# Adding the first level of a sum over keys on VectorE, in the second layer's recurrences alone

## The chip, the cores and the metric

One core of a Trainium2 chip runs the whole kernel. The metric is the device time in microseconds (us) of one launch; the table below gives the median of three runs. PE is TensorE's matmul side, PEld its weight loads, DVE VectorE, ACT ScalarE, POOL GpSimd.

## What is computed

Four layers run over x of shape 16 x 128 x 256 (16 sequences of 128 steps, 256 channels). The first and third are RWKV blocks, the second and fourth attend to a context of 128 positions. The part that the change touches is the recurrence of the RWKV block, with 32 heads of 8 keys s by 8 values t:

```
def step(s, inp):
    k_l, v_l, w_l, r_l = inp
    a = k_l[..., :, None] * v_l[..., None, :]
    out = jnp.einsum('bhs,bhst->bht', r_l, faaaa * a + s)
    s_new = a + w_l[..., None] * s
    return (s_new, out)
_, outs = jax.lax.scan(step, s0, seq)
```

The output of a step is a sum over the 8 keys of r times the state. After it come a group norm, a gate, the projection `Wo` and the block's channel mix.

## The kernel before

The 16 sequences are worked in four groups of four. `STEPS` lists eight steps: the first kernel layer (one RWKV block and one attention) for groups 0 to 3, then the second kernel layer for groups 0 to 3. In the second, the recurrence's unit is of kind `mixer_ffn` and the attention's unit is of kind `attn_mlp`; "the second layer" below is always this second half, some 504 to 1008 us of the profiled span, with a tail of attention and MLP behind it.

Each step is cut into three programs that run side by side, like a software pipeline: `head` (norm, token shift, projections of the next unit), `recurrence` (of this unit) and `attn` (of the unit before). They share the engines. Every engine runs its instructions strictly in the order in which they were issued, and that order is a table: `ORDER` holds for each engine a string of the letters H, R and A, and `in_order` takes the next piece (up to a `yield`) of the head, recurrence or attention program for each letter. So a piece that waits holds back all pieces behind it on its engine.

A recurrence unit has 128 partitions for 4 sequences x 32 heads. It works through the 8 values in `NCH` = 4 chunks of `DC` = 2 values. For each chunk c:

- VectorE forms the outer product k*v in `A_[c % 2]` (`outer`, L473, 128 x 2032),
- runs two scans over key and time, `S_` = w*S + A (L563, 128 x 1024 each),
- multiplies by r: `A_[c % 2]` = `R_` * `S_` (L571, 128 x 2048), and raises `r_rs`;
- TensorE waits for `r_rs` and adds the 8 keys up in PSUM: `RS` = 8 matmuls with the identity (L1301, 128 x 256 each), then raises `r_y`. Each such fp32 matmul stands in the trace as two instructions.

The outer product of chunk c+2 waits for `r_y`, since it writes the same buffer. After the last chunk ScalarE squares the result (L913), VectorE forms the group norm's sums and scales (L585, L588, L590, L592), TensorE transposes (L1079) and projects with `Wo` (L1129).

Beside the recurrence lies attention: TensorE makes the scores of 16 jobs per unit in two alternating banks (L1380), VectorE takes their negative maximum (`nmax`, L659), ScalarE the exponentials (L1003), TensorE transposes them (L1393) and forms the values (L1404). It begins with the queries, which VectorE scales (L654) and a DMA spreads into `QX`. GpSimd makes the reciprocal standard deviations of the layer norms (L767, L768) for VectorE's L421 and the copy L513 before it, and one product of the recurrence (L786).

Of the kernel before, what the change touches and what calls it, by code (L numbers as in the profile page):

```python
# [8 lines left out]
ALU = mybir.AluOpType  # L9
# [11 lines left out]
RH, RS = 32, 8  # L21
# [8 lines left out]
DC = 2  # L30
# [69 lines left out]
for _group in range(G):  # L100
# [2 lines left out]

ORDER = {
    "VectorE":
        "HHHHHHHHHHHHAHHRRHHRRRRRRRRRRRHRHHRRRHHRHHHRRRRHHRRAAHHAARRHAAHAAARARRHHARRAARRAARARRARAAHRAHAARAHRR"
        "HAAAHARRRARRHAHHAARARAAHHAAHHAAAHHRARAARRRRAARRAARARAHARAHRAAARRAARRRHAHAAHRHHRRHAARHHRAARHAHRAAAAAH"
        "HAAAHHRARHHRAARHHRHRAHHARAHRHAHARARARRRARAHHAARRRAAAAHHAARRRRARAHHRRARAAAARAAHHRRRRAAARAHHRHAARHHRRA"
        "RRRAARARRAAHRAHRRRRAHHARARRARAHHARRAAAAAHHRAARRAAARARRRAARRARAAHHARARRARRAHARHAARRHRAAHAHRRRRARAAHHR"
        "RRARAHHARRAAHHAARHHRRRRRRAAARRAARAARAARARAHHAARRHAHARAAAHRRRHHAAAARHHARRRAARAHHARRARHHRRRHRRRAAHRAAA"  # L110
        "RRARARAARARARARARARRARAAARRRAAAHHRARRRAHRHARHRARRARRAHHAHRRAAAAAAAHAAHAHAAAAAAAAAAAAAAAHHHAAAAH",
    "GpSimd":
        "HRRHAARRHAARRHAARHRARAHRRRARHRARAHRARARRHRAHAHHA",
    "ScalarE":
        "HHHHHHHHHHHRRRHHRRHRHRHHHHAHHAAAAHHRAAAAAAAAAAARAAAAHAAAAAARAAAAARAHARAAARAAHAARAAAAAHHHAHHAAAHHHAHR"
        "AAAAAAAARAAAAAAAAAAAAAAAAARHAAARRHARAHAARHAAHAAAAAAAHHHAAAHHHRAHAHAAAHAHAAAAARAAAAAHAAHAAARAAAAAHHHA"
        "AAARRARAHHARAAAAAAAAARHHAAAHAAAHRAAAHRAAAAARAAARARAAHHARHAAAAAHHAAAARAHHAAAARAARRAAAAAAHRHAAAAAAAAAA"
        "ARAAAAAHAAARAAAAAHRAARARAHRAAAAHHAAARAHAAHHAAARHRHRAAARHHAAAAAAAAAAARAAAAAAAHAAAAAAAARAAAHRRAHAAARAH"
        "AAAAARAAHHAHHARRAHHAAARRRAAHAHAAAAAAAAAAAAARAAAAAAARAAARAAARARAHAARAAAHAHHAAARRRARAAHAAHAAAAHAAAAAAA"
        "AAAAAAAAAAHAAAAAAHHAAAAAAAAAAAAHAHAAAAHA",  # L120
    "TensorE":
        "HHHHHHHHHHHHHHHHHHHHHHHRHRRRRRRHRRRRHRRRRRRHHHHHRHRHHRHHHHAHHAHAHAAAHHAAHHAHAHAAAAHRRARAAAARRAAHAAAA"
        "RRAAARARAAAAARRRRAAAAHAARRRRAAHHAAAAAHRHARRAHAAAHHHAHHAAHAHAAHHHHAHHAAAAAAAHRHRAARAAHRHAAAAARAAAARAA"
        "HRARAAAAAHRAAARRAARRRRRRHAAHHAHHARHAHAHAHARAAARAHAHAAHAHAAHHAHHHHAHHHHAHHAAAAHRARHHAHAHARAAARHAAAAAA"
        "RARHRARARHHARAAAARRAHHRAHAAHAARRRRAAHHAAHARHAARARAAAAHAHHHHHAAAAARRARHHAAAHRRAARARAHRHAARHRRRARAAHAA"
        "RRARRAAAHAAAHRHAHRRHAAAHAAHHRAAHHAAAARAAHARHAARRAARAHAHAAAAAHAAAHHAARHRAARRAAAAAHAAAARHARARRRRRAAAAR"
        "ARAAHARRRRAHAAAHARHHRRAAHAHAHAHARAHAHAHAAHRRRAHHRRHAHAAHHAAAAAAAAAHRHRARRAHAAAARHAARAAAAAAAHHARRARAA"
        "AAARRAARAAHAARRRRRHHAHAHAAHAAAHARARAHAHRAHHAHAHAHRAHRRARHAHRRAAAHAHAAAAAAAARRAAARRAAHAAAARAARARAHRHA"
        "ARAHRARRRAAAAARRRRAHAAHAARAARRHAHAHHRHHAAHARRRARAAAHAAARAHHAAHAHAHAAHAAAAAAAAAAAAAAAHAAAAAHAHAAAAAHH"
        "HAAAAAAAHAAAHAHAHHAHAAAAAAHH",  # L130
}


# [17 lines left out]
def build(nc, x, ctx, ctx_t, s0, state, mask_row, mask_col, rwkv_w, attn_w, mlp_w, bias_w, common, out):  # L151
# [5 lines left out]
    with ExitStack() as stack:  # L157
        def sb(name, shape, dt=F32):
            return stack.enter_context(nc.sbuf_tensor(name, [P] + shape, dt))
# [149 lines left out]
        sem = {n: stack.enter_context(nc.semaphore(n)) for n in names}  # L309
# [10 lines left out]
        with nc.Block() as block:  # L320
# [78 lines left out]
            def _(dve):  # L399
                v = nc.vector  # L400
# [146 lines left out]
                def recurrence(u):  # L547
                    xf = X2[u.lane][:].rearrange("p b c -> p (b c)")
                    yield
                    dve.wait_ge(sem["r_turned"], u.at("r_turned", 6))  # L550
                    link(outer(u, 0))
                    yield
                    link(outer(u, 1))
                    yield
                    dve.wait_ge(sem["r_rk"], u.at("r_rk", 1))
                    v.tensor_reduce(RU[:], YT[:].rearrange("p k t -> p t k"), AX.X, ALU.add).then_inc(sem["r_ru"], 1)
                    for c in range(NCH):
                        yield
# [12 lines left out]
                        v.tensor_tensor(A_[c % 2][:], R_[:].unsqueeze(1).broadcast_to([P, DC, RS, T]), S_[:], ALU.mult)\  # L571
                            .then_inc(sem["r_rs"], 1)
                        dve.wait_ge(sem["r_rs"], u.at("r_rs", c + 1))
                        if 1 <= c < NCH - 1:
                            yield
                            last = outer(u, c + 1)
                            if c == NCH - 2:
                                last.then_inc(sem["r_out"], 1)
                                dve.wait_ge(sem["r_out"], u.at("r_out", 1))
                            else:  # L580
                                link(last)

# [24 lines left out]
                    if u.kind == "mixer_ffn":
                        yield from channel_mix(u, "g", in_mixer, 1)
# [463 lines left out]
            def _(pe):  # L1072
# [211 lines left out]
                def recurrence(u):  # L1284
                    pb = lambda h: PB[:, h * 512:(h + 1) * 512]
                    for c in range(NCH):
                        if c == NCH - 1:
                            yield
                            pe.wait_ge(sem["r_vr"], u.at("r_vr", 1))
                            for h in range(HALF):  # L1290
                                last = t.matmul(pb(h), ident, V_[:, h * RS // 2:(h + 1) * RS // 2], start=False, stop=False,
                                                skip_group_check=True)
# [2 lines left out]
                        yield  # L1295
                        pe.wait_ge(sem["r_rs"], u.at("r_rs", c + 1))
                        y = PB[:, DC * c * T:DC * (c + 1) * T]
                        for k in range(RS):
                            if k and k % 2 == 0:
                                yield  # L1300
                            last = t.matmul(y, ident, A_[c % 2][:, :, k], start=(c % 2 == 0 and k == 0), stop=False,  # L1301
                                            skip_group_check=True)
# [273 lines left out]
```

## Time and profile before

| | before |
|---|---|
| median of three runs | 1144.96 us (1141.52 to 1145.21) |
| the profiled execution's own time | 1146.65 us |
| its span | 1144.7 us |
| TensorE matmul busy | 1032.4 us (90% of the span) |
| TensorE weight loads busy | 774.9 us (68%) |
| VectorE busy | 780.4 us (68%) |
| ScalarE busy | 536.1 us (47%) |
| GpSimd busy | 109.5 us (10%) |
| mean granted TensorE clock | 0.966 |

Busy is the time in which at least one instruction of the engine ran. The span is the time from the first to the last instruction of the profiled execution; 1.95 us of that execution's time lie around it.

### The profile page before, as it was taken

How to read it: one execution, taken by the hardware profiler on the slowest of the kernel's cores; microseconds unless marked ns; L12 is line 12 of the kernel's file. 1: busy time of each engine (PE TensorE's matmuls, PEld its weight loads, DVE VectorE, ACT ScalarE, POOL GpSimd, SP SyncE). 2: the span in 40 equal slices, each digit the busy share in tenths (PEclk: the TensorE clock that was granted, in tenths of full speed). 3: DMA queues.
4: the chain of work that ended last, by engine and by line, in shares of the span. 5: the costliest groups of instructions: out<-in, count | busy, mean ns of one | idle time of the engine just before them, and what ended most of it. 6: DMA issues, size and time to landing. Idle time of an engine off the chain costs nothing. (4 is left out here: it accounts for less than half of the span.)

```text
span 1144.7 us, 21376 instructions
## 1 busy us (share of the span) xinstructions
PE 1032.4 (90%) x8866; PEld 774.9 (68%) x8866; DVE 780.4 (68%) x1078; ACT 536.1 (47%) x1643; POOL 109.5 (10%) x101
## 2 busy tenths in 40 slices
PE   7846889989998889978999989998999979999998
PEld 5634567766676657765667667785777757787777
DVE  3597759866996589779975688746986479532330
ACT  1102326743655235552476446642672445734762
POOL 1001010101010020002100202010100010000000
PEclk9967999989999899999999989999999989999999
DMA  9200000000000010000000000001000010000000
GB/s 371 87 0 1 2 25 16 1 2 20 21 2 2 1 32 10 1 2 19 17 6 2 20 20 2 2 2 41 9 1 2 11 38 3 1 1 21 27 10 19
DMA packets 17058, 24.80 MB, mean 22 GB/s; under 512 B 4417, under 2 KB 13761, under 8 KB 16322
## 3 DMA queue, kind: packets, MB, share of 16 engines
q1 hardware_dynamic: 16962, 23.44, 6.2%
q8 instruction: 70, 1.15, 0.4%
q14 instruction: 26, 0.21, 0.1%
HBM read 17.13 MB, written 2.10 MB: 17 GB/s over the span
## 5 line engine op out<-in xcount | busy, mean ns | idle before, releaser
L1003 ACT ACTIVATE big<-QB,nmax 128x128 f32<-128x128 f32 x512 | 181.6, 376 | 110.4 <-DVE nmax L659 109.2
L1301 PE MATMUL PB<-A,common_w 128*128 128x256 f32 x512 | 132.0, 399 | 21.7 <-DVE A L571 21.7
L563 DVE TENSOR_TENSOR_SCAN S_<-W_,A 128x1024 f32<-128x1024 f32 x64 | 146.5, 2311 | 0.3
L1380 PE MATMUL QB<-big,QX 128*128 128x256 f32 x512 | 135.7, 388 | 10.7 <-DMA QX<-big 10.7
L1301 PEld LDWEIGHTS PB<-A,common_w 128*128 128x128 f32 x512 | 97.8, 199 | 43.2 <-DVE A L571 26.7
L659 DVE TENSOR_REDUCE nmax<-QB 128x4 f32<-128x512 f32 x128 | 86.2, 683 | 54.0 <-PE QB L1380 52.7
L1380 PEld LDWEIGHTS QB<-big,QX 128*128 128x128 f32 x512 | 99.9, 196 | 30.3 <-DMA QX<-big 12.2
L1003 ACT ACTIVATION_READ_ACCUMULATOR big<-QB,nmax 128x1 f32 x512 | 110.2, 215 | 0.0
L1267 PE MATMUL PA<-X,rwkv_w 128*32 128x128 f32 x3072 | 100.9, 289 | 10.1 <-DVE X L458 9.8
L449 DVE SCALAR_TENSOR_TENSOR PA<-PA,rwkv_w,SX 128x512 f32<-128x512 f32 x80 | 56.5, 752 | 70.3 <-PE PA L1184 65.5
L1267 PEld LDWEIGHTS PA<-X,rwkv_w 128*32 128x32 f32 x3072 | 88.4, 117 | 22.3 <-DVE X L458 15.6
L1393 PE MATMUL QA<-common_w,big 128*128 128x128 f32 x512 | 78.6, 276 | 3.6 <-ACT CN L1012 2.2
L1393 PEld LDWEIGHTS QA<-common_w,big 128*128 128x128 f32 x512 | 60.8, 141 | 24.7 <-issue 16.3
L473 DVE TENSOR_TENSOR A<-K_,V_ 128x2032 f32<-128x2032 f32 x32 | 72.4, 2263 | 2.1 <-PE PB L1301 1.7
L571 DVE TENSOR_TENSOR A<-R_,S_ 128x2048 f32<-128x2048 f32 x32 | 73.2, 2287 | 0.6
L1375 PE MATMUL QB<-mrow,first_row 128*128 128x512 bf16 x128 | 49.8, 389 | 9.1 <-ACT big L1003 7.4
L1012 ACT ACTIVATE XT<-QA 128x512 f32<-128x512 f32 x64 | 38.7, 605 | 29.0 <-PE QA L1393 28.8
L458 DVE TENSOR_TENSOR X<-PA,XN 128x512 f32<-128x512 f32 x80 | 51.5, 685 | 1.2
L1184 PE MATMUL PA<-low,rwkv_w 32*128 32x256 f32 x256 | 44.8, 425 | 7.3 <-ACT K_ L892 1.9
L1129 PE MATMUL QA<-attn_w,CT 128*128 128x256 f32 x192 | 45.3, 382 | 4.5 <-DVE CT L678 4.5
L1012 ACT ACTIVATE CN<-QA 128x512 f32<-128x512 f32 x64 | 38.8, 606 | 20.1 <-PE QA L1393 19.8
L1129 PE MATMUL PB<-rwkv_w,S_ 128*128 128x256 f32 x192 | 45.4, 385 | 1.1 <-DVE S_ L598 1.0
(192 smaller groups left out, 1720.4 us busy)
## 6 DMA issues: line engine op xcount, KB each, us to landing
rwkv_w<-in_rwkv_w SPq DMA_DIRECT2D x2, 2866.0 KB, 14.9
QX<-big SPq DMA_DIRECT2D x128, 32.0 KB, 1.9
attn_w<-in_attn_w SPq DMA_DIRECT2D x2, 1031.5 KB, 17.2
mlp_w<-in_mlp_w SPq DMA_DIRECT2D x1, 2052.0 KB, 23.4
X<-in_x SPq DMA_DIRECT2D x4, 512.0 KB, 16.8
ctx<-in_ctx SPq DMA_DIRECT2D x4, 512.0 KB, 3.4
ctx<-in_ctx_t SPq DMA_DIRECT2D x4, 512.0 KB, 3.4
out<-XT SPq DMA_DIRECT2D x4, 256.0 KB, 2.0
```

What stands on the lines that cost most here:

```text
L449: last = v.scalar_tensor_tensor(pa4(h), pa4(h), r_pack[u.layer][:, col:col + 1], SX[:, h], ALU.add, ALU.mult)
L473: return v.tensor_tensor(A_[c % 2][:, :, :, 1:T], K_[:, :, 0:T - 1].unsqueeze(1).broadcast_to([P, DC, RS, T - 1]), V_[:, DC * c:DC * c + D ...
L563: last = v.tensor_tensor_scan(S_[:, d].rearrange("p k t -> p (k t)"), W_[:].rearrange("p k t -> p (k t)"), A_[c % 2][:, d].rearrange("p k ...
L571: v.tensor_tensor(A_[c % 2][:], R_[:].unsqueeze(1).broadcast_to([P, DC, RS, T]), S_[:], ALU.mult)\
L659: v.tensor_reduce(nmax[:, n % 2], bank(2 + n % 2).rearrange("p (j s) -> p j s", j=JH), AX.X, ALU.max, negate=True).then_inc(sem["a_max"], 1)
L1003: last = s.activation(PR[:, n % 2, j], bank(2 + n % 2)[:, j * T:(j + 1) * T], ACT.Exp, bias=nmax[:, n % 2, j:j + 1], accum_out=den[:, b, h ...
L1012: s.activation(PT[n % QUAD], bank(0).rearrange("p (j t) -> p j t", j=JH), ACT.Copy)\
L1129: last = t.matmul(dst[:, (b - base) * C:(b - base + 1) * C], lhs(h, b), w[:, h], start=(h == 0 and b == 2 * k), stop=(h == HALF - 1 and bi ...
L1267: last = t.matmul(PA[RH * b:RH * b + RH, k * T:(k + 1) * T], wt[:, h, RH * k:RH * k + RH], src[:, h, b * T:(b + 1) * T], start=(h == 0), s ...
L1301: last = t.matmul(y, ident, A_[c % 2][:, :, k], start=(c % 2 == 0 and k == 0), stop=False, skip_group_check=True)
L1380: last = t.matmul(o, QX[b % 2][:, i, h], K2[:, :, h, b * T:(b + 1) * T], start=False, stop=True, skip_group_check=True)
L1393: last = t.transpose(bank(0)[:, j * T:(j + 1) * T], PR[:, n % 2, j], ident)
```

## The change

In units of kind `mixer_ffn`, VectorE adds keys 4 to 7 to keys 0 to 3 in place, behind the product with r, and only then raises `r_rs`. TensorE then adds 4 keys instead of 8. All other units stay as they were. The new addition stands behind a `yield` of its own, so that the table can put other pieces between the product and it.

```diff
-                        v.tensor_tensor(A_[c % 2][:], R_[:].unsqueeze(1).broadcast_to([P, DC, RS, T]), S_[:], ALU.mult)\
-                            .then_inc(sem["r_rs"], 1)
+                        last = v.tensor_tensor(A_[c % 2][:], R_[:].unsqueeze(1).broadcast_to([P, DC, RS, T]), S_[:], ALU.mult)
+                        if u.kind == "mixer_ffn":
+                            link(last)
+                            yield
+                            part = A_[c % 2]
+                            last = v.tensor_tensor(part[:, :, 0:RS // 2], part[:, :, 0:RS // 2], part[:, :, RS // 2:RS], ALU.add)
+                        last.then_inc(sem["r_rs"], 1)
                         dve.wait_ge(sem["r_rs"], u.at("r_rs", c + 1))
...
-                        for k in range(RS):
+                        for k in range(RS // 2 if u.kind == "mixer_ffn" else RS):
                             if k and k % 2 == 0:
                                 yield
                             last = t.matmul(y, ident, A_[c % 2][:, :, k], start=(c % 2 == 0 and k == 0), stop=False,
```

`link` raises VectorE's own semaphore and waits for it, so the addition starts when the product has been written.

The strings of `ORDER` are new on every engine that has one, in the first layer too. Their first line for VectorE:

```diff
     "VectorE":
-        "HHHHHHHHHHHHAHHRRHHRRRRRRRRRRRHRHHRRRHHRHHHRRRRHHRRAAHHAARRHAAHAAARARRHHARRAARRAARARRARAAHRAHAARAHRR"
...
+        "HHHHHHHHHHAHHHHRRHHRRRRRRRRRRRHRHHRRRHHRHHHRRRRHHRRAAHHAARRHAAHAAARRRRHARAHARARAARRARARAHAARHAAHRRR"
...
```

The string of VectorE is 16 letters longer (595 to 611) and that of TensorE 32 shorter (828 to 796): 16 additions more, and two pieces of two matmuls less in each of the 16 chunks. Three places show what the new order does. Names of lines behind L575 are 5 higher in the changed kernel (`nmax` is L664 there, the matmuls over keys L1306); its addition is L576.

VectorE, the end of group 3's recurrence in the second layer. Before:

```order
L563 SCALAR_TENSOR_TENSOR S_<-W_,A 128x1024
L571 TENSOR_TENSOR A<-R_,S_ 128x2048
L671 RECIPROCAL rden<-den 128x32
L473 TENSOR_TENSOR A<-K_,V_ 128x16x127
L659 TENSOR_REDUCE nmax<-QB 128x4
L678 TENSOR_TENSOR CT<-QA,az 128x2x2x128
L659 TENSOR_REDUCE nmax<-QB 128x4
L563 SCALAR_TENSOR_TENSOR S_<-W_,A 128x1024 x2
L571 TENSOR_TENSOR A<-R_,S_ 128x2048
L687 TENSOR_TENSOR X<-QA,X 128x512
```

Now:

```order
L571 TENSOR_TENSOR A<-R_,S_ 128x2048
L576 TENSOR_TENSOR A<-A 128x2x512
L676 RECIPROCAL rden<-den 128x32
L473 TENSOR_TENSOR A<-K_,V_ 128x16x127
L664 TENSOR_REDUCE nmax<-QB 128x4
L683 TENSOR_TENSOR CT<-QA,az 128x2x2x128
L664 TENSOR_REDUCE nmax<-QB 128x4
L563 SCALAR_TENSOR_TENSOR S_<-W_,A 128x1024 x2
L571 TENSOR_TENSOR A<-R_,S_ 128x2048
L692 TENSOR_TENSOR X<-QA,X 128x512
L664 TENSOR_REDUCE nmax<-QB 128x4
L576 TENSOR_TENSOR A<-A 128x2x512
```

Here the update of X (L687, now L692) and one more `nmax` stand ahead of the last addition, and otherwise only the additions are new.

VectorE, the start of group 2's recurrence in the second layer (its first scans, and the start of attention beside it). Before:

```order
L571 TENSOR_TENSOR A<-R_,S_ 128x2048
L563 SCALAR_TENSOR_TENSOR S_<-W_,A 128x1024
L654 TENSOR_SCALAR big<-QA,attn_w 128x512 x2
L563 SCALAR_TENSOR_TENSOR S_<-W_,A 128x1024
L659 TENSOR_REDUCE nmax<-QB 128x4 x2
L571 TENSOR_TENSOR A<-R_,S_ 128x2048
L659 TENSOR_REDUCE nmax<-QB 128x4 x2
L473 TENSOR_TENSOR A<-K_,V_ 128x16x127
```

Now:

```order
L576 TENSOR_TENSOR A<-A 128x2x512
L421 TENSOR_SCALAR az<-X,amv,arstd 128x256 x4
L563 SCALAR_TENSOR_TENSOR S_<-W_,A 128x1024 x2
L659 TENSOR_SCALAR big<-QA,attn_w 128x512 x2
L571 TENSOR_TENSOR A<-R_,S_ 128x2048
L576 TENSOR_TENSOR A<-A 128x2x512
L664 TENSOR_REDUCE nmax<-QB 128x4 x2
L473 TENSOR_TENSOR A<-K_,V_ 128x16x127
```

The second chunk's scans now stand ahead of the scaling of the queries (`big`), and its product and addition ahead of the first two `nmax`.

VectorE, the second chunk of group 0's recurrence in the second layer. Before:

```order
L416 BN_AGGR amv<-abn 128x2 x4
L563 SCALAR_TENSOR_TENSOR S_<-W_,A 128x1024
L421 TENSOR_SCALAR az<-ctx,amv,arstd 128x256 x4
L545 SCALAR_TENSOR_TENSOR Gt<-Gt,PA 128x1024
L413 BN_STATS bn<-X 128x6 x4
L416 BN_AGGR mv<-bn 128x2 x4
L563 SCALAR_TENSOR_TENSOR S_<-W_,A 128x1024
L513 COPY XN<-st 128x8
L421 TENSOR_SCALAR X_0<-X,mv,rstd 128x256 x4
L654 TENSOR_SCALAR big<-QA,attn_w 128x512 x2
L571 TENSOR_TENSOR A<-R_,S_ 128x2048
```

Now:

```order
L416 BN_AGGR amv<-abn 128x2 x4
L545 SCALAR_TENSOR_TENSOR Gt<-Gt,PA 128x1024
L413 BN_STATS bn<-X 128x6 x4
L416 BN_AGGR mv<-bn 128x2 x4
L421 TENSOR_SCALAR az<-ctx,amv,arstd 128x256 x4
L563 SCALAR_TENSOR_TENSOR S_<-W_,A 128x1024 x2
L513 COPY XN<-st 128x8
L421 TENSOR_SCALAR X_0<-X,mv,rstd 128x256 x4
L571 TENSOR_TENSOR A<-R_,S_ 128x2048
L576 TENSOR_TENSOR A<-A 128x2x512
L659 TENSOR_SCALAR big<-QA,attn_w 128x512
```

Both scans now stand behind the second of two batch-norm blocks and behind L421, and the scaling of the queries behind the product and the addition.

## Rows read from the trace of the kernel before

**Rows 1.** The page, part 1: busy time, share of the span, instructions of each engine.
```profile
PE 1032.4 (90%) x8866; PEld 774.9 (68%) x8866; DVE 780.4 (68%) x1078; ACT 536.1 (47%) x1643; POOL 109.5 (10%) x101
```

**Rows 2.** Groups of instructions: count | busy us, mean ns | idle us before, releaser.
```profile
L1301 PE MATMUL PB<-A,common_w 128*128 128x256 f32 x512 | 132.0, 399 | 21.7 <-DVE A L571 21.7
...
L571 DVE TENSOR_TENSOR A<-R_,S_ 128x2048 f32<-128x2048 f32 x32 | 73.2, 2287 | 0.6
...
L590 DVE TENSOR_TENSOR A<-PB,RU 128x1024 f32<-128x1024 f32 x8 | 9.8, 1225 | 0.3
...
L659 DVE TENSOR_REDUCE nmax<-QB 128x4 f32<-128x512 f32 x128 | 86.2, 683 | 54.0 <-PE QB L1380 52.7
```

**Rows 3.** Windows: the four stretches of the second layer, and 708.40 to 775.00 between two.
```profile
core 0: us, PE busy (x) PEld busy (x) DVE busy (x) ACT busy (x) POOL busy (x), PEclk, DMA share, GB/s
523.28:575.88 52.60, 48.07 (x223) 34.09 (x221) 49.86 (x58) 21.69 (x61) 8.52 (x5) 1.00 0.07 20
653.64:704.64 51.00, 44.11 (x251) 31.45 (x249) 45.48 (x45) 22.87 (x91) 7.50 (x3) 0.93 0.08 21
708.40:775.00 66.60, 65.85 (x777) 51.46 (x776) 41.74 (x67) 36.37 (x96) 6.76 (x6) 1.00 0.01 2
775.05:838.75 63.70, 59.86 (x331) 43.07 (x330) 52.06 (x62) 33.15 (x118) 6.85 (x5) 0.97 0.08 23
924.64:967.44 42.80, 38.94 (x248) 30.36 (x249) 39.51 (x28) 23.93 (x103) 2.36 (x1) 0.92 0.06 13
```

**Rows 4.** The page, part 4: the chain that ended last, by engine and line.
```profile
PE 36%; DVE 5%; ACT 3%; issue 1%; SPq 1%; POOL 1%; DMA 1%; POOLq 0%; DVEq 0%; ACTq 0%
PE QB L1380 4%; PE PB L1129 4%; PE PB L1301 3%; PE QA L1129 3%; PE PA L1267 3%; PE QA L1119 2%; PE PA L1109 2%; PE QA L1393 2%; ACT big L1003 2%; PE PA L1119 2%; PE QA L1404 1%; PE PB L1088 1%; PE QB L1109 1%; PE QB L1088 1%; PE PA L1184 1%
```

**Rows 5.** The chain in order of time (start us, us, what), second layer.
```profile
675.90 2.21 DVE A L571
...
702.45 2.21 DVE A L571
...
704.70 3.73 PE PB L1301 x16
...
838.82 3.72 PE PB L1301 x16
...
960.46 1.73 PE PB L1301 x8
...
968.88 3.47 PE PB L1301 x16
```

**Rows 6.** Timeline of VectorE, group 3: start, us, what [idle before <-releaser].
```profile
929.27 0.69 DVE L659 TENSOR_REDUCE nmax<-QB 128x4 f32<-128x512 f32 x1 [2.35 <-PE QB L1380]
...
965.15 2.29 DVE L571 TENSOR_TENSOR A<-R_,S_ 128x2048 f32<-128x2048 f32 x1
...
969.02 0.69 DVE L687 TENSOR_TENSOR X<-QA,X 128x512 f32<-128x512 f32 x1 [1.57 <-PE QA L1094]
```

**Rows 7.** Timeline of VectorE, group 1.
```profile
665.86 0.69 DVE L659 TENSOR_REDUCE nmax<-QB 128x4 f32<-128x512 f32 x1 [1.79 <-PE QB L1380]
...
671.96 0.69 DVE L659 TENSOR_REDUCE nmax<-QB 128x4 f32<-128x512 f32 x1 [2.48 <-PE QB L1380]
...
700.99 0.17 DVE L513 COPY XN<-st 128x8 f32<-128x8 f32 x1 [0.90 <-POOL rstd L768]
```

**Rows 8.** Timeline of VectorE, group 0.
```profile
538.86 1.38 DVE L421 TENSOR_SCALAR az<-ctx,amv,arstd 128x256 f32<-128x256 f32 x4 [1.12 <-POOL arstd L768]
...
546.46 0.17 DVE L513 COPY XN<-st 128x8 f32<-128x8 f32 x1 [1.18 <-POOL rstd L768]
```

**Rows 9.** Timeline of VectorE, group 2.
```profile
783.71 1.38 DVE L421 TENSOR_SCALAR az<-X,amv,arstd 128x256 f32<-128x256 f32 x4 [1.41 <-POOL arstd L768]
...
798.48 0.69 DVE L659 TENSOR_REDUCE nmax<-QB 128x4 f32<-128x512 f32 x1 [3.74 <-PE QB L1380]
...
802.91 0.69 DVE L659 TENSOR_REDUCE nmax<-QB 128x4 f32<-128x512 f32 x1 [3.73 <-PE QB L1380]
```

More of the change, by code:

```diff
@@ L105 @@
     "VectorE":
-        "HHHHHHHHHHHHAHHRRHHRRRRRRRRRRRHRHHRRRHHRHHHRRRRHHRRAAHHAARRHAAHAAARARRHHARRAARRAARARRARAAHRAHAARAHRR"
[L107 to L110, printed above, removed]
@@ L111 @@
-        "RRARARAARARARARARARRARAAARRRAAAHHRARRRAHRHARHRARRARRAHHAHRRAAAAAAAHAAHAHAAAAAAAAAAAAAAAHHHAAAAH",
+        "HHHHHHHHHHAHHHHRRHHRRRRRRRRRRRHRHHRRRHHRHHHRRRRHHRRAAHHAARRHAAHAAAARRRRHARAHARARAARRARARAHAARHAAHRRR"
+        "AAHHARARHRARARHHARRAAAAHHAAHHAAAHHARRAARRRRAARARARARAAHHARRARAARAARRRHHAAHARHHHRARRHHRAAAHHARRAAAAAH"
+        "HAAAHHRARHHRAARHHRHRAHHARHAARAHHARRRARARAARHHRAAARRAAHHAARRRRARAHHRRARAAAARAAHHRRRRRAAAHHARRHRRAHARH"
+        "RRRRARAARRARRAARAHHRRRARHHARRRARAAAHHAARRAAAHHARRRAAAARARRRAAHRAHRRAARRRAARRRAARRHRAAHRHAARRRAHAHRRR"
@@ L112 @@
+        "RAARHHARRRARHHAARAHHRAAAHHRRRRRRRRAARARRAARRAARARAHAHRRAARHARAAHRAAARHRAARHHARAHRHAARRARAHHARRARRHHR"
+        "RRARAHAHRRAARRARARRARARARRARARARARRARAAARRRAARAHHRARRRAHRHAHRRRRAARRHHHAARRAAAAAAAAHAHAAAHAAAAAAAAAA"
+        "AAHHAHAAAAH",
     "GpSimd":
-        "HRRHAARRHAARRHAARHRARAHRRRARHRARAHRARARRHRAHAHHA",
+        "HRRHAARRHAARRHAARHRARAHRRRARHRARARHARARRHRHAAHHA",
     "ScalarE":
-        "HHHHHHHHHHHRRRHHRRHRHRHHHHAHHAAAAHHRAAAAAAAAAAARAAAAHAAAAAARAAAAARAHARAAARAAHAARAAAAAHHHAHHAAAHHHAHR"
@@ L116 @@
[L116 to L120, printed above, removed]
@@ L121 @@
-    "TensorE":
[L122 to L130, printed above, removed]
+        "HHHHHHHHRHHHRRHHRHRRHRHHHHAHHAAAAHHRAAAAAAAAAAAAARAAAAHAAAAAAARAAHAARRAARAHAARAAAAAAHAHAHHHAAAHHHRAH"
@@ new lines @@
+        "AAAAAAAAAAAAAAAARAAAAAAARAAAARHRAHARAHAARHHAAAAAAAAHAHRHAAAHHHHAAHAAAHAAAAHAAAAARAHAAHAAAAAAARAAAAHR"
+        "HHAARARHHAAARAAAAAAARHAHAAAHAAHRAHAARAAAAAAARARAARAAAHHRHAAAAAHHAAAAARHHAAARAARARAAAHAHAAARAAAAAAAAA"
+        "AARAAHAAAAAARAHRAAAARAARAHRAAHAHAAARHAAHHAAAAHRARHRHAHAARAAAAAAAARAAAAAAAHAARAAAAAAAAAAAAHAARRAHRAAA"
+        "AAAHRAAHAHAHHARAARAARRHHAAAHRHAAAAAAAAAAAARAAAAAAARAAAAARAAARRAHARAAAAHAHHAAARRHAARRAAAAHAAAHAAAAAAA"
+        "AAAAAAAAAAHAAAAAAHHAAAAAAAAAAAAHAHAAAHAA",
@@ new lines @@
+    "TensorE":
+        "HHHHHHHHHHHHHHHHHHHHHHHRRRRHRRRRHRRHRRRRRRRHHHHHRHRHHRHHHHAHHAAHAHAAHHAAAAHHAHAHARRRAAARHAAAAARRAAAA"
+        "AHAARAARAARAARRAARHAAAARRRRRHHAAAAAHARAHRARAHAAAHHHAHHAAHAHAAHHHHAHHAAAHAAAARRAHRAAHAARAHAAAAAAARHAA"
+        "RARRAARRAARRRAAAHAAARRRRHAHHAAHHARHAHAARAHAHAARAHAHAHAAHAAHHAHHHHAHHHHAHHAAAAHAHHAAARRAAHAHAAARRHAAR"
+        "ARRHAAHARAHAARAARHHRAAARARAAHRHRRRAHHAAAAHRAAHRARAAAAHAHHHHHAAAAAHRRHAAAHAARHHHAHARAAAARARRAAAARRAAA"
+        "AAHAHRHAHRRHHAAAAAHARAAHAAAHHRAARARHAHAAARRAHHAHAAAAHAAHAAHAAARRAAAAHRRAAHAAAAAAAAARRHARAAARRAAAHAAH"
+        "ARHHRAHRHAAHAAHRAAHHHAHRAHHAARAHRHRRAHHAAAAAAAAAAARAARHHAAHHAAARAAAHHAARAAAAAAAAAAARRAAAAAHRRRHHAAHH"
+        "AAAAAHARHARHAAHRAHHAHAHAARAHRRRAAHRHRAHAAHHAAAAAAAARAAARAAAAHAAARRAAAAAARHAHRAHAAAARRRAAAHHARAARARHA"
+        "HHAHHHARAHARRHRHAHAAAARRAAAAAHAHAHAAHAAAAAAAAAAAAAAAAAHAAAHAHAAAAAHHHAAAAAAAHAAAAHHAHHHAAAAAAHAH",
```

## Prediction

> **What bounds the kernel now.** I began with the busy times [rows 1]: TensorE 90% of the span, VectorE 68%. Taken alone they say that TensorE is the bound and VectorE has room. The chain of waits says the same [rows 4]: TensorE holds 36% of the span there, VectorE 5%; all engines together make 48%, since this chain could be followed back through the later half only. The matmuls over keys (L1301) are 3% of the span on it, some 34 us, and that half is the second layer with its tail. But an average is taken over stages with different limits, so I looked at the stretches in which the change works. I call the time from a recurrence's first scan to its last product with r its **stretch**, and cut the trace there [rows 3]: the first, second, fourth and fifth rows are groups 0, 1, 2 and 3. The reader is to see that VectorE is busy 49.9 of 52.6 us, 45.5 of 51.0, 52.1 of 63.7 and 39.5 of 42.8, hence 95%, 89%, 82% and 92%, and TensorE 91%, 86%, 94% and 91%. In these stretches both engines are nearly full. Between two of them only TensorE is: 65.9 of 66.6 us in the third row [rows 3], VectorE 41.7. So outside the stretches TensorE sets the pace, and a stretch that ends later pushes all that is behind it; inside, whichever is fuller after the change does.
>
> **What TensorE loses.** 4 units x 4 chunks x 4 matmuls = 64 matmuls, which are 128 of the 512 instructions of the group L1301 [rows 2]. At full clock 16 instructions take 3.47 us and 8 take 1.73 [rows 5], so a chunk saves 1.73 us, a unit 6.9 and the four units 27.7 us. That is the most the change can give.
>
> **What VectorE gains.** 16 additions of 128x1024. None is in the trace. From below: half of the product's 2.29 us, 1.14. From above: the whole 2.29, if writing in place slowed it [rows 2]. Nearest is L590, a tensor_tensor of the same 128x1024: 1.225 us [rows 2]; I take 1.2, so 4.8 us a unit and 19.2 in all. The wait of `link` ahead of it I cost at nothing: between scans and product the same kind of wait stands, and that group has 0.6 us of idle before it over 32 products [rows 2]. No DMA moves.
>
> **What of it lies on the path.** In a stretch VectorE had 2.7, 5.5, 11.6 and 3.3 us of idle (span less busy) [rows 3]. The additions can only hide in that. I walked the new order of each stretch with the old durations.
>
> Group 3. Of its idle, 2.35 us stand before the first `nmax`, which waits for scores that wait for the queries' DMA [rows 6]; the order there is as before, so this stays. The other 0.9 us can go. The order shows two more pieces ahead of the last addition, the update of X and one `nmax`, 0.69 and 0.67 us long [rows 6, 2] but following each other at some 0.6 us, beside the 4.8 us of additions. The last addition then ends at 4.8 + 1.3 - 0.9 = 5.2 us past 967.44, where the last product ended. TensorE started its last chunk at 968.88, 1.4 us behind the product, being busy itself, and ended at 972.35 [rows 5]. Now it starts at 972.6 and needs 1.73: it ends at 974.4, **+2.0 us**, although it did 6.9 us less.
>
> Group 1. Its idle is 1.79 and 2.48 us before two `nmax` and 0.90 before the copy that waits for GpSimd's deviations [rows 7]. The new order fills the second; the first grows by what is put in front of it, and the third by as much as the block of batch norm moves back. I take 0.4 us less idle in all. With one more `nmax` (0.67 us a piece) [rows 2] the last addition ends 4.8 + 0.6 - 0.4 = 5.0 us late, and the last chunk, which started right at the product's end and took 3.73 us [rows 5], gives 1.73 back: **+3.3 us**. The chain runs through VectorE's products here, three of the four (the first and the last stand in [rows 5]), which says that VectorE already set this stretch.
>
> Group 0. Both waits for GpSimd, 1.12 and 1.18 us [rows 8], are filled: the new order has the second batch-norm block ahead of the first `az`, and a pair of scans ahead of the copy. One `nmax` fewer lies in the stretch. So 4.8 - 2.3 - 0.6 = 1.9 us, less 1.73 for the last chunk, 0.2; but the scaling of the queries now stands behind a product and an addition, and attention starts later by about 3 us, of which I charge 0.8: **+1.0 us**.
>
> Group 2. It has holes: 1.41 us for GpSimd, then 3.74 and 3.73 us before the first two `nmax` [rows 9]. The new order puts the first addition into the first hole and the second chunk's product and addition (3.5 us) into the next. The last addition then ends where the last product did, and the last chunk (3.72 us) [rows 5] gives 1.73 back: **-1.7 us**.
>
> The sum is 2.0 + 3.3 + 1.0 - 1.7 = +4.6 us. Against the profiled execution's own 1146.65 us (span 1144.7, 1.95 around it) that is 1151.3; that execution is 1.7 us above the median of the runs shown, so I give 1144.96 + 4.6 = **1149.6 us**. The order in the first layer is new as well; its additions and matmuls are the same in number, I see no wait that it clearly removes, and cost it at 0, with 3 us to either side.
>
> [...]
>
> **The rivals.**
>
> *TensorE sets the end in the stretches too (faster).* For it: the chain holds matmuls over keys at the end of groups 1, 2 and 3 [rows 5], and TensorE is busy 94% and 91% there; the new order puts additions into holes. Then half of the 34 us on the chain goes, 17 us, and only group 1's three products carry an addition on the chain, 3.6 us: 13.4 us faster, 1131.6. With half of that, where VectorE gives way in some stretches, 1138. Against it: VectorE is as full, and has no way to do 6 us more in 3.3 us of idle. [...]
>
> *It balances (no change).* The holes cover more than I think, above all group 1's GpSimd wait, or the new order of the first layer gives 3 us: 1142 to 1148.
>
> *The additions delay attention (slower by more).* Each `nmax` behind an addition comes 1.2 us later; ScalarE and TensorE's scores wait for it in two alternating banks. Its place is the start of attention beside each recurrence; it decides if the holes before `nmax` stay as long as before. Then all 19.2 us of additions lie on the path and only the last chunks' 4 x 1.73 = 6.9 come back: +12.3, 1157. TensorE, idler, may also drop its clock more often: it was 0.93 and 0.92 in groups 1 and 3 [rows 3]. With an addition priced at the upper bound of 2.29 us my own sum would be +17 higher, 1167, which I hold for hardly possible.
>
> **How the numbers follow.** A measurement can tell this kernel's change from none at about 0.3%, 3.4 us. Chances: my forecast 0.33, of which its spread of some 4 us leaves a part below 3.4 us; attention delayed 0.12; balance 0.20; TensorE the bound in full or in part 0.35. That gives 0.42 for slower, 0.23 for no change and 0.35 for faster. The cases have both signs: the forecast's own range is 1145 to 1155; the range that holds 8 in 10 has to reach the faster case's 1131.6 and most of the slower one's, 1131 to 1157.
>
> **What would show each step.** Right: an addition of 1.2 us; stretches of about 54, 56, 64 and 48 us, with VectorE above 90% in groups 0, 1 and 3; TensorE busy about 1005 us, and its idle before the matmuls over keys (L1306), released by VectorE, well above the 21.7 us of before [rows 2], by some 20 us; waits for GpSimd in group 0 gone. Wrong: stretches of groups 2 and 3 no longer than before, or TensorE's idle as before and the span some 15 us shorter, which would say that VectorE's rows could be packed closer than I walked them. If the additions took over 1.5 us, the price is wrong, not the place.

## The result, and the profile after

| | before | changed |
|---|---|---|
| median of six runs | 1145.09 us (1141.12 to 1145.67) | 1152.21 us (1150.32 to 1156.02) |
| ratio | | 1.0073, 95% interval 1.0059 to 1.0087 |
| profiled execution, span | 1144.7 us | 1150.0 us |
| mean granted TensorE clock | 0.966 | 0.961 |

The change makes the kernel slower by 0.7%; the forecast was 1149.6 us, slower by 0.4%. The page of the changed kernel, to be held against [rows 1]:

```profile
span 1150.0 us, 21144 instructions
...
PE 1012.0 (88%) x8738; PEld 753.7 (66%) x8738; DVE 797.1 (69%) x1094; ACT 536.4 (47%) x1643; POOL 104.8 (9%) x101
```

TensorE is busy 20.4 us less and VectorE 16.7 more. (27.7 us of matmuls at full clock were taken out; where the clock is low, an instruction's time grows, and overlapping times are counted once.) Only now read the windows. The stretches, from a recurrence's first scan to its last addition, stand here as in [rows 3], groups 0 to 3:

```profile
core 0: us, PE busy (x) PEld busy (x) DVE busy (x) ACT busy (x) POOL busy (x), PEclk, DMA share, GB/s
523.50:578.90 55.40, 47.22 (x204) 32.06 (x203) 54.76 (x62) 22.00 (x61) 4.86 (x5) 0.94 0.07 19
655.42:710.64 55.22, 39.87 (x203) 27.23 (x205) 50.89 (x50) 23.15 (x90) 5.42 (x3) 0.88 0.07 19
778.84:843.55 64.71, 57.33 (x318) 40.77 (x316) 57.52 (x68) 32.90 (x122) 7.52 (x5) 0.97 0.08 22
926.77:975.27 48.50, 36.06 (x230) 26.45 (x230) 45.70 (x34) 25.19 (x110) 2.35 (x1) 0.96 0.05 12
```

They take 55.4, 55.2, 64.7 and 48.5 us where they took 52.6, 51.0, 63.7 and 42.8: +2.8, +4.2, +1.0 and +5.7, together 13.7 us. VectorE is busy 99%, 92%, 89% and 94% of them, TensorE 85%, 72%, 89% and 74%. The engine that bounds the stretches is VectorE in groups 0, 1 and 3; in group 2 the two are level, and only the experiments tell.

What lies between them, and the tail behind the last, before:

```profile
575.88:653.64 77.76, 73.77 (x856) 56.30 (x857) 48.31 (x84) 47.10 (x147) 8.58 (x6) 1.00 0.02 4
704.64:775.05 70.41, 69.60 (x792) 54.71 (x793) 45.48 (x73) 39.13 (x107) 6.76 (x6) 1.00 0.01 2
838.75:924.64 85.89, 81.74 (x825) 59.67 (x824) 48.88 (x85) 40.44 (x99) 7.53 (x8) 1.00 0.03 11
967.44:1144.70 177.26, 169.21 (x981) 136.43 (x979) 58.89 (x125) 92.71 (x287) 7.86 (x16) 1.00 0.04 13
sum 411.32, PE 394.32 PEld 307.11 DVE 201.57 ACT 219.38 POOL 30.74; mean PE 98.58 PEld 76.78 DVE 50.39 ACT 54.85 POOL 7.68
```

and after:

```profile
578.90:655.42 76.52, 72.54 (x852) 54.80 (x853) 48.49 (x83) 46.16 (x147) 8.59 (x6) 1.00 0.02 5
710.64:778.84 68.20, 66.94 (x797) 52.16 (x790) 44.83 (x71) 38.76 (x106) 7.97 (x6) 1.00 0.01 2
843.55:926.77 83.22, 79.61 (x817) 58.21 (x816) 47.74 (x83) 40.84 (x96) 7.53 (x8) 1.00 0.04 12
975.27:1150.00 174.73, 166.13 (x965) 133.94 (x965) 57.70 (x123) 91.55 (x282) 7.72 (x16) 1.00 0.04 13
sum 402.67, PE 385.23 PEld 299.11 DVE 198.76 ACT 217.31 POOL 31.82; mean PE 96.31 PEld 74.78 DVE 49.69 ACT 54.33 POOL 7.95
```

This sum is 8.6 us shorter, and TensorE's busy time in it 9.1 us shorter. So outside the stretches the relief of TensorE comes back as time, nearly one for one. With the first scan 0.22 us later (523.50 against 523.28), 13.7 - 8.6 + 0.2 = 5.3 us, the whole difference of the spans. Those 0.2 us are no measure of the first layer's new order: in the seven kernels below whose first layer is that of before the first scan stands at 521.4 to 522.9 us, and in the four others that have the new order at 518.6 to 524.3.

The groups of the addition and of the matmuls over keys, as in [rows 2]:

```profile
L1306 PE MATMUL PB<-A,common_w 128*128 128x256 f32 x384 | 96.7, 392 | 18.4 <-DVE A L571 16.2
...
L576 DVE TENSOR_TENSOR A<-A 128x1024 f32<-128x1024 f32 x16 | 19.5, 1220 | 0.4
```

The addition takes 1.220 us, and the wait of `link` leaves 0.4 us of idle over all 16. The 128 instructions are gone (512 to 384), but the idle before the rest did not grow as the prediction said it would: 18.4 us where it was 21.7, and nearly all of both lies in the first layer (2.3 and 2.5 us in the second, in the lines below). TensorE's idle went elsewhere. Its longest waits in the second layer (504 to 1008 us; total us, times, longest), changed kernel:

```profile
PE QB L1380 <- ACT big L1008: 19.2, 21, 3.4
PE QB L1385 <- DMA QX<-big: 11.3, 3, 3.8
...
PE PB L1306 <- DVE A L576: 2.3, 3, 1.8
```

and before:

```profile
PE QB L1380 <- DMA QX<-big: 9.8, 3, 3.8
...
PE PB L1301 <- DVE A L571: 2.5, 3, 1.5
PE QB L1375 <- ACT big L1003: 2.5, 5, 1.2
```

The mask row that opens a job's scores (L1380 now, L1375 before) waits 19.2 us in all, 21 times, for the exponentials of two jobs earlier, and waited 2.5. TensorE often reached a score before attention was ready for it.

Group 1's holes of [rows 7] in the changed kernel:

```profile
667.73 0.69 DVE L664 TENSOR_REDUCE nmax<-QB 128x4 f32<-128x512 f32 x1 [2.73 <-PE QB L1385]
...
702.60 0.17 DVE L513 COPY XN<-st 128x8 f32<-128x8 f32 x1 [1.11 <-POOL rstd L773]
```

The hole before the first `nmax` grew from 1.79 to 2.73 us, the second is gone, and the wait for GpSimd went from 0.90 to 1.11. Group 0's two waits for GpSimd [rows 8] are gone. In group 3 the hole of [rows 6] stayed at its 2.35 us:

```profile
931.40 0.69 DVE L664 TENSOR_REDUCE nmax<-QB 128x4 f32<-128x512 f32 x1 [2.35 <-PE QB L1385]
```

and TensorE, which had started its last chunk there 1.4 us behind the product, now waits for the last addition:

```profile
975.33 1.99 PE L1306 MATMUL PB<-A,common_w 128*128 128x256 f32 x8 [1.80 <-DVE A L576]
```

### The profile page after: what moved, and what is told of

Its sections match the earlier page's. It is cut to its first block, busy times and chain, and to the rows that moved or that the text cites. A ratio compares the mean times of both kernels' runs of the same rounds, so it can differ in the third digit from the quotient of the medians.

```text
span 1150.0 us, 21144 instructions
## 1 busy us (share of the span) xinstructions
PE 1012.0 (88%) x8738; PEld 753.7 (66%) x8738; DVE 797.1 (69%) x1094; ACT 536.4 (47%) x1643; POOL 104.8 (9%) x101
## 4 chain that ended last, share of the span: by engine, by line
PE 58%; DVE 27%; ACT 6%; issue 4%; POOL 2%; DMA 2%; SPq 1%; DVEq 0%; POOLq 0%; ACTq 0%
DVE S_ L563 7%; PE PA L1272 7%; PE QB L1385 5%; PE PB L1134 5%; PE QA L1134 5%; DVE A L571 4%; PE PB L1306 3%; PE QA L1398 3%; PE PA L1189 3%; ACT big L1008 3%; PE QB L1093 2%; PE PA L1114 2%; PE QA L1124 2%; DVE A L473 2%; DVE nmax L664 2%
## 5 line engine op out<-in xcount | busy, mean ns | idle before, releaser
L1385 PE MATMUL QB<-big,QX 128*128 128x256 f32 x512 | 138.0, 394 | 12.2 <-DMA QX<-big 12.2
L664 DVE TENSOR_REDUCE nmax<-QB 128x4 f32<-128x512 f32 x128 | 86.6, 683 | 51.8 <-PE QB L1385 50.5
L1385 PEld LDWEIGHTS QB<-big,QX 128*128 128x128 f32 x512 | 101.7, 199 | 30.4 <-DMA QX<-big 13.5
L1306 PE MATMUL PB<-A,common_w 128*128 128x256 f32 x384 | 96.7, 392 | 18.4 <-DVE A L571 16.2
L1306 PEld LDWEIGHTS PB<-A,common_w 128*128 128x128 f32 x384 | 72.8, 196 | 36.2 <-DVE A L571 19.3
L1380 PE MATMUL QB<-mrow,first_row 128*128 128x512 bf16 x128 | 50.5, 395 | 26.0 <-ACT big L1008 24.0
## 6 DMA issues: line engine op xcount, KB each, us to landing
X<-in_x SPq DMA_DIRECT2D x4, 512.0 KB, 16.9
```

Of the source, the lines that this page charges most:

```text
L664: v.tensor_reduce(nmax[:, n % 2], bank(2 + n % 2).rearrange("p (j s) -> p j s", j=JH), AX.X, ALU.max, negate=True).then_inc(sem["a_max"], 1)
L1385: last = t.matmul(o, QX[b % 2][:, i, h], K2[:, :, h, b * T:(b + 1) * T], start=False, stop=True, skip_group_check=True)
```

## The experiments

Twelve kernels. "Old order" is the order of every engine in the kernel before, "new order" that of the changed kernel. **Theory A** is the prediction's: VectorE sets the stretches, and TensorE's relief counts only outside them. **B**: the new order costs the time. **C**: TensorE sets the end everywhere. Effects in us are the ratio's excess times 1144 us. The diffs are shortened; in the new order they are shown against the changed kernel, in the old order against the first of the experiments, the change whole. What is said of stretches comes from one traced execution of each kernel.

### The change split, in the old order

The change whole, with the addition inside its product's piece and TensorE's four matmuls in the first two of the four old pieces:

```diff
                         if u.kind == "mixer_ffn":
                             link(last)
-                            yield
                             part = A_[c % 2]
```

> The addition and the halved sum over keys, but every engine in the order of the kernel before (the addition right behind its product, TensorE's four matmuls in the first two of the four old places). If VectorE's time in the recurrences sets the end (theory A), the change costs here at least what it costs in its own order, since nothing is moved into the holes: 19.2 us of additions less some 6.9 us for the last chunks and a few us of idle, 1152 to 1158 us. If the new order is what costs (theory B), this kernel is at the time of before or below, 1140 to 1146. If TensorE sets the end (theory C), 1125 to 1138.

Measured: ratio 1.0083 (1.0065 to 1.0101), **+9.5 us**, 1153.7 us. B falls: the change costs in the old order what it costs in its own (+8.4, the intervals overlap). C falls by its sign. In the trace the four stretches take 223.5 us together where they took 210.1, and the time between and behind them is 5.2 us shorter (406.2 against 411.3).

The additions alone, with TensorE still adding all 8 keys (keys 4 to 7 count twice, so the result isn't that of the reference):

```diff
-                        for k in range(RS // 2 if u.kind == "mixer_ffn" else RS):
+                        for k in range(RS):
```

> The additions are made but TensorE still adds all 8 keys, in the order of before: keys 4 to 7 are counted twice in the second layer, so this prices the additions alone. Theory A: 12 to 17 us above before, 1157 to 1162. Theory C (VectorE has room, TensorE sets the end): under 5 us above before, up to 1150.

Measured: 1.0143 (1.0127 to 1.0158), **+16.4 us**. Of 19.5 us of additions 16.4 show. VectorE, busy 68% of the span, had little room where they stand. The four stretches take 225.2 us together, 15.1 more than before, and the time between and behind them is as it was (411.4 against 411.3).

The relief alone, which leaves keys 4 to 7 out of the sum:

```diff
-                        if u.kind == "mixer_ffn":
-                            link(last)
-                            part = A_[c % 2]
-                            last = v.tensor_tensor(part[:, :, 0:RS // 2], part[:, :, 0:RS // 2], part[:, :, RS // 2:RS], ALU.add)
```

> Only the relief: TensorE adds keys 0 to 3 in the second layer and keys 4 to 7 are left out, no addition, order of before. It prices what 27.7 us less TensorE work are worth. Theory A: the last chunks' 6.9 us and little more, 5 to 11 us below before, 1134 to 1140. Theory C: 17 to 27 us below before, 1118 to 1128.

Measured: 0.9956 (0.9940 to 0.9971), **-5.0 us**, 1138.9 us. Taking 27.7 us of work from an engine that is busy 90% of the span gives 5 us. Its stretches:

```profile
521.52:575.22 53.70, 45.65 (x195) 31.14 (x194) 49.94 (x58) 20.51 (x60) 8.50 (x5) 0.94 0.07 19
652.48:703.18 50.70, 39.35 (x227) 26.70 (x225) 45.46 (x45) 22.65 (x91) 7.50 (x3) 0.93 0.08 21
772.38:832.64 60.26, 53.66 (x307) 37.19 (x306) 52.58 (x62) 33.33 (x118) 6.84 (x5) 1.00 0.08 24
917.88:960.66 42.78, 36.54 (x229) 27.00 (x230) 39.76 (x28) 23.87 (x103) 2.35 (x1) 0.92 0.06 13
```

53.7, 50.7, 60.3 and 42.8 us against 52.6, 51.0, 63.7 and 42.8: TensorE falls to 85%, 78%, 89% and 85%, VectorE stays at 93% in group 3, and only group 2's stretch becomes clearly shorter. The same kernel shows what the wait for the exponentials is:

```profile
PE QB L1382 <- ACT big L1007: 13.5, 18, 2.8
```

13.5 us of it, without one addition, where the kernel before has 2.5. So that wait is mostly where a relieved TensorE stands idle in the stretches; it is not made by late `nmax` alone.

### The same three in the new order

The new order with the computation of the kernel before (8 matmuls a chunk in the two pieces, an empty piece for the addition):

```diff
-                        for k in range(RS // 2 if u.kind == "mixer_ffn" else RS):
-                            if k and k % 2 == 0:
+                        for k in range(RS):
+                            if k and k % (RS // 2 if u.kind == "mixer_ffn" else 2) == 0:
                                 yield
```

> The computation of the kernel before (no addition, 8 matmuls a chunk) in the new order of every engine. Theory A: the order costs little by itself, 1143 to 1149. Theory B: it carries the loss, 1150 to 1154.

Measured: 1.0148 (1.0128 to 1.0168), **+16.9 us**, 1161.6 us. A miss, well above what even B allowed. With all 8 matmuls, in two pieces of four where the old order has four of two, the work between the stretches and behind them, in the same four windows, becomes

```profile
sum 418.86, PE 401.54 PEld 312.68 DVE 201.43 ACT 222.63 POOL 31.80; mean PE 100.39 PEld 78.17 DVE 50.36 ACT 55.66 POOL 7.95
```

418.9 us with TensorE busy 401.5, against 411.3 and 394.3 before. The sums of the stretches are 218.4 against 210.1 us. Without the change this is a poor order; with it, it is level with the old one. It suits the halved matmuls.

The change with all 8 matmuls kept, and the change without its additions, both in the new order (edits as above):

> The change in its own order, but TensorE adds all 8 keys (keys 4 to 7 counted twice in the second layer). Against the changed kernel's 1152.2 us it prices the relief in the new order. In the old order the relief was worth 5 us. If its worth doesn't depend on the order (theory D: two fixed prices), 1157 us and no more than 1160. If the new order was fitted to fewer matmuls, so that TensorE sets the end there where the work is not halved (theory E), 20 us or more above the changed kernel, over 1170.

Measured: 1.0199 (1.0181 to 1.0217), **+22.8 us**, 1166.9 us. Between the two answers that I had given.

> The new order with TensorE's 4 matmuls a chunk and no additions: keys 4 to 7 are left out. Against the changed kernel it prices the additions in the new order. In the old order they cost 15 us. Theory D: 1137 us. Theory E (the new order hides additions in VectorE's holes, as the prediction walked it: 4.8 us of 19.2 plus what waits remain): 1140 to 1146.

Measured: 0.9947 (0.9926 to 0.9968), **-6.1 us**, 1139.0 us, below the 1140 to 1146 that I gave if the new order hid additions in VectorE's holes: they cost what they cost in the old order. What is hidden of them, some 5 of 19.5 us, is hidden in either order.

| us against before | neither | relief alone | additions alone | both |
|---|---|---|---|---|
| old order | 0 | -5.0 | +16.4 | +9.5 |
| new order | +16.9 | -6.1 | +22.8 | +8.4 |

With the relief in place the additions cost 14.5 us in either order. The relief is worth 5 to 7 us in the old order and 14 to 23 in the new one, since the new order needs it. Read the columns "both" and "relief alone": the new order is worth about 1 us, within the measurement, and even free additions would have given only 5 to 6.

### More VectorE work in the new order

```diff
                             last = v.tensor_tensor(part[:, :, 0:RS // 2], part[:, :, 0:RS // 2], part[:, :, RS // 2:RS], ALU.add)
+                            link(last)
+                            last = v.tensor_tensor(part[:, :, 0:RS // 2], part[:, :, 0:RS // 2], part[:, :, RS // 2:RS], ALU.subtract)
+                            link(last)
+                            last = v.tensor_tensor(part[:, :, 0:RS // 2], part[:, :, 0:RS // 2], part[:, :, RS // 2:RS], ALU.add)
```

> The changed kernel in its own order with the addition followed by a subtraction and the addition again: two more instructions of 1.22 us a chunk on VectorE, 39 us in all, same sum. Theory A: VectorE sets all four stretches by now and nearly all of it shows, 33 to 42 us above the changed kernel's 1152.2, 1185 to 1194. If VectorE still had room in the stretches, less than half of it, under 1172.

Measured: 1193.5 us, **41.3 above the changed kernel** for 32 x 1.225 = 39.2 us of work. The groups and the stretches:

```profile
L580 DVE TENSOR_TENSOR A<-A 128x1024 f32<-128x1024 f32 x16 | 19.6, 1225 | 0.5
L578 DVE TENSOR_TENSOR A<-A 128x1024 f32<-128x1024 f32 x16 | 19.6, 1225 | 0.5
L576 DVE TENSOR_TENSOR A<-A 128x1024 f32<-128x1024 f32 x16 | 19.5, 1220 | 0.4
```

```profile
524.25:589.59 65.34, 48.82 (x204) 33.56 (x202) 64.44 (x70) 21.98 (x61) 4.86 (x5) 0.92 0.06 17
666.09:731.54 65.45, 42.21 (x215) 27.98 (x213) 60.70 (x58) 24.89 (x99) 5.43 (x3) 0.87 0.06 16
800.22:872.11 71.89, 58.48 (x318) 41.47 (x316) 67.23 (x76) 35.18 (x127) 8.49 (x5) 0.95 0.07 20
956.53:1015.11 58.58, 40.93 (x230) 29.59 (x230) 55.49 (x42) 26.05 (x112) 2.36 (x1) 0.85 0.04 10
```

The stretches grew by 9.9, 10.2, 7.2 and 10.1 us for 9.8 us of instructions each: no VectorE room is left in three of them, and 2.6 us of it in group 2. The rest of the 41.3 lies outside them, 3.3 us of it between and behind, and these runs don't explain it.

### One group alone, one chunk alone, in the old order

The same condition stands at TensorE's `range(RS // 2 ...)`. Group 2 (in a second kernel `== 3`):

```diff
-                        if u.kind == "mixer_ffn":
+                        if u.kind == "mixer_ffn" and u.group == 2:
```

> The change in group 2 of the second layer alone, order of before. Theory A says a recurrence pays what its VectorE idle doesn't cover. Group 2's stretch had 11.6 us of idle, so its 4.8 us of additions hide and the relief of its TensorE, which was 94% busy, shows: 0 to 3 us below before, 1141 to 1144. If each recurrence pays alike (a quarter of the 9.5 us that all four paid in this order), 1146.5.

> The change in group 3 alone, order of before. Its stretch had 3.3 us of VectorE idle, 2.35 of it fixed by the queries' DMA. Theory A: 4 to 5 us longer, 1.7 to 2 back by the last chunk, 2 to 3.5 us above before, 1146 to 1148. If each recurrence pays alike, 1146.5 (then this and group 2 alone don't differ).

Measured: group 2 alone 1.0011 (0.9999 to 1.0022), **+1.3 us**; group 3 alone 1.0026 (1.0014 to 1.0038), **+3.0 us**. Group 3 is as expected: its stretch grew by 4.7 us and the time behind it shrank by 1.7. Group 2 is cheaper, but the intervals overlap, and the gain I expected isn't there. Its additions did hide: the stretch took 64.3 us, 0.6 more than before. But the time behind it shrank by 0.1 us only, and in the traced execution its last chunk shows a reason. Timeline of TensorE, then two windows around it (columns as above, the granted clock is the third number from the end):

```profile
838.22 3.59 PE L1308 MATMUL PB<-A,common_w 128*128 128x256 f32 x8 [2.12 <-DVE A L575]
```

```profile
832.00:838.20 6.20, 4.10 (x18) 2.48 (x16) 6.10 (x5) 2.16 (x3) 0.00 (x0) 1.00 0.01 3
838.20:842.00 3.80, 3.78 (x10) 3.05 (x11) 3.76 (x6) 0.15 (x1) 0.00 (x0) 0.55 0.00 0
```

TensorE, ahead of its work now, waited 2.12 us for the addition, having been busy 4.10 of the 6.20 us ahead, and the granted clock fell to a mean of 0.55, its lower level of 1.2 GHz for nearly all of the chunk. The 8 instructions took 3.59 us; the 16 of before took 3.72 [rows 5]. The halved sum gave nothing back. But the wait alone doesn't decide it. With the change whole in the old order the same chunk follows the same wait, with 4.06 of the 6.17 us ahead busy, and keeps the full clock:

```profile
842.77 1.99 PE L1308 MATMUL PB<-A,common_w 128*128 128x256 f32 x8 [2.12 <-DVE A L575]
```

```profile
836.60:842.77 6.17, 4.06 (x18) 2.44 (x16) 6.07 (x5) 2.12 (x3) 0.00 (x0) 1.00 0.00 0
842.77:844.76 1.99, 1.99 (x8) 1.44 (x8) 1.96 (x4) 0.00 (x0) 0.00 (x0) 1.00 0.00 0
```

What lowered it in the one and not in the other these runs don't tell, nor whether the other executions of group 2 alone lost it too. In the changed kernel itself this didn't happen at the last chunks (1.89 to 1.99 us each); the clock of group 1's stretch fell from 0.93 to 0.88 and of group 0's from 1.00 to 0.94, and that of group 3's rose from 0.92 to 0.96.

The last chunk of the second layer's recurrences (in a second kernel `c == NCH - 1` alone, so in all eight recurrences):

```diff
-                        if u.kind == "mixer_ffn":
+                        if u.kind == "mixer_ffn" and c == NCH - 1:
```

> Addition and half sum in the last chunk of each second-layer recurrence alone, in the order of before. If only the last chunk's relief reaches the end, as the prediction has it, this keeps nearly all of the gain (1.73 us a unit) for a quarter of the additions (1.2 us a unit): 1.5 to 4 us below before, 1140 to 1142.5. If the relief is worth the same in every chunk (5 us over 16 chunks) and an addition 1 us, it is 2 to 3 us above before, 1146 to 1147.

> The same in the last chunk of all eight recurrences, the first layer's too, where TensorE waits more often. If the last chunk's relief reaches the end there as well: 3 to 7 us below before, 1137 to 1141; if not, the time of the kernel with the second layer's last chunks alone, or 1 to 4 us above it.

Measured: 1.0017 (1.0007 to 1.0027), **+1.9 us**, and with the first layer 1.0024 (1.0014 to 1.0035), **+2.7 us**. Both expectations of a gain fell. The stretches grew by 1.3, 1.5, 2.3 and 1.3 us for 1.2 us of addition, and the time behind each shrank by 1.6, 0.6, 0.7 and 1.2, not 1.73. Group 2's stretch is no fine measure: the second kernel, which does the same there, took 62.8 us at a granted clock of 1.00, the first 66.0 at 0.97. In group 1 the clock is again part of it, 8 instructions in 3.12 us after a wait of 1.93:

```profile
705.41 3.12 PE L1308 MATMUL PB<-A,common_w 128*128 128x256 f32 x8 [1.93 <-DVE A L575]
```

### The additions on GpSimd

```diff
+                    def add(c):
+                        pool.wait_ge(sem["r_pr"], u.at("r_pr", c + 1))
+                        part = A_[c % 2]
+                        q.tensor_tensor(part[:, :, 0:RS // 2], part[:, :, 0:RS // 2], part[:, :, RS // 2:RS], ALU.add).then_inc(sem["r_rs"], 1)
```

VectorE's product raises a semaphore of its own, `r_pr`; GpSimd's additions stand in its queue in the order in which the products came in the trace of before.

> The four additions of each second-layer recurrence on GpSimd (10% busy) instead of VectorE, all other engines in the order of before. GpSimd's product of the same 128x1024 took 2.36 us. If VectorE's occupancy alone is what the additions cost, this is near the relief alone plus 4 x 1.2 us for the slower last addition: 1141 to 1146. If operations of GpSimd slow VectorE's beside them (a scan beside V_'s product took 3.41 us where others take 2.28), or TensorE's and GpSimd's queues wait for the longer addition, over 1150.

Measured: 1.0184 (1.0166 to 1.0203), **+21.0 us**, 1166.6 us: the dearest place for them. Groups of the addition and of VectorE's outer product, and TensorE's wait for it:

```profile
L788 POOL TENSOR_TENSOR A<-A 128x1024 f32<-128x1024 f32 x16 | 44.7, 2793 | 155.5 <-DVE A L572 155.5
...
L474 DVE TENSOR_TENSOR A<-K_,V_ 128x2032 f32<-128x2032 f32 x32 | 78.2, 2445 | 2.3 <-PE PB L1317 1.8 <-ACT V_ L905 0.3
```

```profile
PE PB L1317 <- POOL A L788: 31.2, 13, 4.8
```

An addition takes 2.35 us at the median, up to 4.43, and TensorE waits for 13 of the 16, 31.2 us in all. The outer product took 2.263 us on average before and 2.445 now, 5.8 us over its 32. So the price of an addition is not VectorE's occupancy alone: where TensorE comes to wait for it, its length counts. How the 21 us divide between the waits, the slower neighbours and the clock (0.951) these runs don't tell.

## Why the prediction was right, point by point

- **VectorE bounds the stretches.** Right. They took 55.4, 55.2, 64.7 and 48.5 us; forecast were about 54, 56, 64 and 48. The additions alone lengthen the stretches by 15.1 us, and what lies outside them not at all, and two further instructions a chunk show 41.3 us for 39.2. For group 2 it holds only in part: it hid 2.6 of 9.8 us even then.
- **The price of an addition**, 1.2 us: 1.220.
- **The stretches one by one.** Group 0, +1.9: +2.8. Group 1, +5.0: +4.2. Group 2, 0: +1.0. Group 3, +5.2: +5.7. Together +12.1: +13.7. Of the fixed holes, 2.35 us stayed, and group 0's waits for GpSimd went. In group 2 VectorE's idle fell from 11.6 to 7.2 us, but its busy time grew by 5.5, not 4.8, and the wait for GpSimd that the first addition was to fill is still 1.25 us.
- **What comes back behind them**, in all some 7.5 us (four times 1.73, and 1.4 that TensorE was behind in group 3, less 0.8 for attention): 8.6 us in the trace. The sum fits; the reason given, the last chunk's own matmuls, is too narrow. With the last chunks alone the time behind the stretches shrank by 4.1 us in all, not 6.9, and with the change whole in the old order by 5.2. The rest may come from TensorE reaching the stretch's end with less of its queue left, which suits the new order better; no run separates it.
- **Group by group** the net in the trace is +1.6, +2.0, -1.7 and +3.2 us for groups 0 to 3, where +1.0, +3.3, -1.7 and +2.0 were forecast. Group 2's net is right by luck: its stretch grew by 1.0 and 2.7 came back behind it. The errors of groups 1 and 3 cancel each other. The group alone, in the old order, isn't the faster case that the step implied.
- **The first layer at 0**: neither borne out nor refuted, since the first scan moves by more than the difference of 0.2 us between kernels with the same first layer.
- **The sum**, +4.6: +5.3 between the two spans, +7.1 between the medians, +8.4 by the ratio (+6.7 to +10.0). The trace of before is of an execution 1.6 us above its median and the trace of after is of one at its own (1152.17 us), so 1.6 us of the difference between +5.3 and +7.1 is the choice of execution. The size was forecast too small: +4.6 lies below the ratio's interval. The time itself, 1149.6 against 1152.2 us, is met within 0.3%, but of the change only 55 to 65% was forecast. By the kernels that split the change, the additions cost more of their 19.5 us (14.5 to 16.4) than the walked +12.1 and 0.8 for attention.
- **TensorE's busy time**, about 1005 us: 1012.0. It fell by 20.4 us, not 27.7.
- **The sign of the idle** was wrong: it did not grow before the matmuls over keys (21.7 to 18.4 us) but before the scores (2.5 to 19.2). I had looked for the idle where the new dependency is. In this kernel TensorE waits at whichever piece of its order is ready last, here attention's.
- **What the averages said.** By matmul busy time, 90%, TensorE was the engine to relieve, and taking 27.7 us from it gave 5. The Trainium skill, Perfetto Trace Analysis, "Identifying the Most-Contended Engine", wants TensorE's headroom judged not by matmul busy time but by the rate of its arithmetic and the busy share of its weight loads. The trace agrees as far as it goes: weight loads were level with VectorE at 68%, which names neither engine. The number that decided was no average, but the busy share in the stretch.

The rival that TensorE sets the end is refuted by the relief alone, the rival of balance by the interval of the ratio. The rival that attention is delayed, +12.3 us, lies above the interval as the forecast lies below it. Its mechanism is there, but as the smaller part: with the relief alone, in the old order, the wait for the exponentials is already 13.5 us, of 19.2 in the changed kernel. That the new order did the harm is refuted: it is level with the old one. An order better than both isn't excluded.

No kernel here that computes the same beats the one before. The nearest is the one with group 2 alone, +1.3 us, whose interval (0.9999 to 1.0022) includes no change.

## What to carry to other kernels

Before moving work from a full engine to a half-empty one, cut the trace at the stage where the work stands and compare the two engines there: 68% on average was 82 to 95% in place. Then ask what the relief is worth by itself, with a kernel that leaves the work out; here it was worth 5 us of 27.7, so even additions for nothing would have gained no more than 5 to 6 us, and on VectorE they cost 14.5. And an order of instructions belongs to the work that it orders: tested with the matmuls put back, the new order was 17 us slow, which says nothing about the change it came with.

## What was not expected of the hardware

- TensorE's clock fell once just behind a wait: 8 instructions took 3.59 us at a granted clock of 0.55 after 2.12 us of idle, where 16 had taken 3.72 at full clock. It doesn't always: after the same 2.12 us at the same place another kernel's 8 took 1.99 us at 1.00.
- GpSimd's fp32 addition of 128x1024 took 2.35 us against VectorE's 1.22, and in one case 4.43 us, with VectorE busy beside it.
- VectorE's addition in place, reading and writing the same rows with a stride of the chunk's halves, took the time of one whose three tiles are different ones: 1.220 us against 1.225 for L590 [rows 2].
